# Two-layer conditioned transformer in float32: layer 1's modulation moved into the set-up, layer 0's feed-forward weights converted behind tile 0's attention, two PSUM banks for the last tile's chunks

## What is computed

```python
def layer0(x, cond):                       # modulated block with gates
    y = layernorm(x) * (1 + cond @ g1_w + g1_b) + (cond @ b1_w + b1_b)
    x = x + attention(y) * tanh(cond @ a1_w + a1_b) * 0.1
    z = layernorm(x) * (1 + cond @ g2_w + g2_b) + (cond @ b2_w + b2_b)
    return x + (gelu(z @ fc1_w + fc1_b) @ fc2_w + fc2_b) * tanh(cond @ a2_w + a2_b) * 0.1

def layer1(x, cond, mask):                 # shift, scale = split(cond @ ada_w + ada_b)
    h = layernorm(x) * (1 + scale1) + shift1
    q, k = rotary(h @ wq + bq), rotary(h @ wk + bk)
    x = x + masked_attention(q, k, h @ wv + bv) @ wo + bo
    h = layernorm(x) * (1 + scale2) + shift2
    return x + gelu(h @ ff_w1 + ff_b1) @ ff_w2 + ff_b2
```

## Time and profile before

| | |
|---|---|
| median of 3 runs | 2088.32 us (2086.74 to 2089.87) |
| the profiled execution | 2085.85 us, span 2084.0 us |
| mean granted TensorE clock | 0.971 of full |
| busy share of the span | PE 89%, PEld 80%, ACT 63%, DVE 60%, POOL 41% |

### The profile page before, as it was taken

One profiled execution on the slowest core, in us unless ns is written; L12 is line 12 of the kernel. 1 busy time (PEld: TensorE's weight loads), 2 busy tenths in 40 slices (PEclk: granted clock), 3 DMA queues, 4 the chain that ended last, 5 costly groups with the idle time before them and its releaser, 6 DMA issues.

```text
span 2084.0 us, 41504 instructions
## 1 busy us (share of the span) xinstructions
PE 1845.1 (89%) x12623; PEld 1664.0 (80%) x12623; DVE 1240.7 (60%) x2973; ACT 1319.0 (63%) x2315; POOL 849.9 (41%) x1036
## 2 busy tenths in 40 slices
PE   4789999999999999997877898888988889888897
PEld 4678888888888888886876888878888788887786
DVE  5566666666666666666653656546655466554651
ACT  3457667776667767775655566666666656656563
POOL 1214333333333333334444445554445544455433
PEclk8899999999999999999998999999999999999999
DMA  6454443333444444343431323223333233332220
GB/s 166 96 128 115 119 121 94 98 98 103 111 117 112 113 121 114 90 103 97 134 92 46 95 83 96 76 75 96 84 92 84 67 96 86 91 86 66 87 62 31
DMA packets 324131, 199.83 MB, mean 96 GB/s; under 512 B 158946, under 2 KB 312548, under 8 KB 324068
## 3 DMA queue, kind: packets, MB, share of 16 engines
q1 hardware_dynamic: 324068, 199.06, 35.7%
HBM read 80.98 MB, written 17.33 MB: 47 GB/s over the span
## 4 chain that ended last, share of the span: by engine, by line
PE 45%; issue 22%; ACT 8%; POOL 6%; DVE 6%; SPq 6%; DMA 5%; POOLq 1%; ACTq 0%; DVEq 0%
PE D L885 10%; PE C L885 9%; PE A L885 7%; PE B L1035 6%; PE B L885 6%; PE B L1021 3%; DMA x_res<-in_x 3%; ACT x_in L682 2%; POOL h_lo L550 2%; SPq L321 2%; ACT hact L739 2%; DMA rotation<-rotation 2%; ACT v_blocks L734 1%; SPq L418 1%; POOL rotation L590 1%
## 5 line engine op out<-in xcount | busy, mean ns | idle before, releaser
L550 POOL TENSOR_TENSOR h_lo<-hact,h_hi 128x512 fp32r<-128x512 f32 x256 | 330.6, 1291 | 341.1 <-ACT h_hi L744 332.6
L885 PE MATMUL D<-wgt_hi,h_hi 128*128 128x256 f32 x1024 | 305.4, 298 | 29.3 <-POOL h_lo L550 22.9
L885 PE MATMUL C<-z_hi,wgt_hi 128*128 128x512 f32 x512 | 218.6, 427 | 106.8 <-ACT hact L739 104.8
L885 PE MATMUL D<-wgt_hi,h_lo 128*128 128x256 f32 x1024 | 291.7, 285 | 0.0
L885 PE MATMUL D<-wgt_lo,h_hi 128*128 128x256 f32 x1024 | 291.2, 284 | 0.0
L885 PE MATMUL A<-k_pad,q_pad 128*128 128x256 f32 x1536 | 259.8, 296 | 12.3 <-DVE exps L1340 5.5
L1035 PEld LDWEIGHTS B<-v_blocks,probs_turned 128*128 128x128 f32 x2048 | 262.2, 201 | 7.1 <-ACT probs_turned L753 2.5
L1035 PE MATMUL B<-v_blocks,probs_turned 128*128 128x68 f32 x2048 | 266.5, 280 | 0.0
L739 ACT ACTIVATE hact<-C,b_col 128x512 f32<-128x512 f32 x256 | 176.4, 689 | 113.7 <-PE C L885 111.3
L1334 DVE TENSOR_REDUCE mx<-A 128x8 f32<-128x512 f32 x256 | 174.3, 681 | 115.7 <-PE A L1007 61.2
L885 PEld LDWEIGHTS D<-wgt_hi,h_hi 128*128 128x128 f32 x1024 | 198.9, 194 | 42.2 <-POOL h_lo L550 20.1
(11 more groups left out here) (138 smaller groups left out, 4258.0 us busy)
## 6 DMA issues: line engine op xcount, KB each, us to landing
k_pad<-k_flat SPq DMA_DIRECT2D x512, 64.0 KB, 2.0
q_pad<-q_flat SPq DMA_DIRECT2D x256, 128.0 KB, 2.3
gates<-gates SPq DMA_DIRECT2D x64, 256.0 KB, 4.3
x_bias<-x_bias SPq DMA_DIRECT2D x32, 512.0 KB, 3.5
rotation<-rotation SPq DMA_DIRECT2D x128, 128.0 KB, 2.1
x_in<-in_x SPq DMA_DIRECT2D x16, 512.0 KB, 3.9
gates<-gated_bias SPq DMA_DIRECT2D x32, 256.0 KB, 4.9
x_res<-in_x SPq DMA_DIRECT2D x16, 512.0 KB, 4.5
```

The lines of the kernel that those rows point to most:

```text
L550: pool.tensor_tensor(hb[1][:, m % 2, :], hact[:, m % 2, :], hb[0][:, m % 2, :].bitcast(F32), ALU.subtract).then_inc(h_lo, 1)
L885: ins = nc.tensor.matmul(dst, l, r, start=first_start and n == 0, stop=last_stop and n == len(todo) - 1, **kw)
```

## The change

Four edits are made together.

1. Layer 1's modulation. SP loads the two `ada` matrices and their eight columns in `begin` (into the last third of `rotation` and into `zn`, free until then), and PE and DVE compute layer 1's scales and shifts in `second`. `third` loses them on SP, PE and DVE.
2. Layer 0's feed-forward weights. SP issues their two loads (1 MB each) in `second` and no longer in `begin`. ACT and DVE convert them in `third`, after step 0, and no longer in `second`. PE waits for them ahead of the first `hidden` and `back` of tile 0 in step 1.
3. Set-up order. ACT converts the weights of queries, keys and values ahead of its wait for the modulation, the projection's right behind; DVE likewise in `begin`; ACT's tanh of the gates stands ahead of tile 1's normalisation; POOL clears `q_pad` in DVE's place.
4. The last tile. Its odd chunks go to bank A[0], and `last_chunks` writes `hidden(m)` ahead of `back(m-1)`; `hidden(m)` waits for the gelu of chunk m-2.

```diff
@@ build
-        ada_raw = [rot[:, n * TE:(n + 1) * TE].rearrange("p (k n) -> p k n", k=KC) for n in range(2)]
+        ada_raw = [buf.rearrange("p (k n) -> p k n", k=KC) for buf in (rot[:, 2 * TE:3 * TE], zn_buf[:, :])]
+        def hidden_bank(tile, m):
+            return A[0] if known(tile) and tile == 2 * NT - 1 and m % 2 else C
@@ SP begin
-                ld(w_in[2], w_raw[1].rearrange("p (k n) -> p k n", k=KC), rows(w[0]["fc1_w"]))
-                ld(w_in[3], w_raw[2].rearrange("p (k n) -> p k n", k=MC), rows(w[0]["fc2_w"]))
                 ld(mask_in, mask_u8[:, :], t["mask_BxS_bf1"])
+                for n in range(2):
+                    ld(mods_in[2], ada_raw[n], rows(w[1][f"ada{n + 1}_w"]))
+                    columns(mods_in[2], 1, n, [w[1][f"ada{n + 1}_b"][D:2 * D], w[1][f"ada{n + 1}_b"][0:D]])
@@ SP second
                 ld(rows_out, mask_rows, mask_add)
+                ld(w_in[2], w_raw[1].rearrange("p (k n) -> p k n", k=KC), rows(w[0]["fc1_w"]))
+                ld(w_in[3], w_raw[2].rearrange("p (k n) -> p k n", k=MC), rows(w[0]["fc2_w"]))
                 sp.wait_ge(rows_out, 80)
@@ SP third
-                sp.wait_ge(w_lo[2], 1)
-                for n in range(2):
-                    ld(mods_in[2], ada_raw[n], rows(w[1][f"ada{n + 1}_w"]))
-                    columns(mods_in[2], 1, n, ...)
                 qk_columns(1, [w[1]["bq"], w[1]["bk"]])
@@ ACT
             def begin():
                 first_norm(0)
+                high_weights(0, 0)
                 act.wait_ge(mod_done, 8)
                 first_columns(0, 0)
-                high_weights(0, 0)
+                high_weights(1, 0)
                 act.wait_ge(bias_in[0], NBIAS[0])
             def second():
-                high_weights(1, 0)
                 act.wait_ge(pe_gates, 1)
                 nc.scalar.activation(hact[:, 1, :], C[:, :], ACT.Tanh).then_inc(gates_tanh, 1)
+                first_norm(1)
+                first_columns(1, 0)
+                act.wait_ge(mod_done, 16)
+
+            def third():
                 high_weights(2, 0)
                 high_weights(3, 0)
-                act.wait_ge(mod_done, 16)
-
-            def third():
                 act.wait_ge(mod_done, 32)
                 act.wait_ge(bias_in[1], NBIAS[1])
@@ PE
             def second():
                 modulations(Dk[1], mod_raw[2], mod_raw[3])
+                pe.wait_ge(mods_in[2], 16 * 10)
+                pe.wait_ge(mod_done, 8)
+                modulations(Dk[0], ada_raw[0][:, :, D:2 * D], ada_raw[0][:, :, 0:D])
                 ...
+                pe.wait_ge(mod_done, 16)
+                modulations(Dk[1], ada_raw[1][:, :, D:2 * D], ada_raw[1][:, :, 0:D])
             def third():
-                ...
-                pe.wait_ge(w_lo[2], 1)
-                pe.wait_ge(w_lo[3], 1)
             def hidden(tile, m):
+                if known(tile) and tile == 2 * NT - 1:
+                    pe.wait_ge(gelu, upto(tile, MC, max(m - 1, 0)))
+                    pe.wait_ge(s_sub, upto(tile, 2 * G, 2 * G))
+                else:
+                    await_(pe, gelu, upto(tile, MC, m))
+            def last_chunks(tile):
+                hidden(tile, 0)
+                hidden(tile, 1)
+                for m in range(2, MC):
+                    back(tile, m - 2)
+                    hidden(tile, m)
@@ DVE
                 modulations(0, 0)
                 low_weights(0, 0)
+                low_weights(1, 0)
             def second():
-                low_weights(1, 0)
                 ...
-                low_weights(2, 0)
-                low_weights(3, 0)
+                dve.wait_ge(mods_in[2], 16 * 10)
+                for n in range(2):
+                    dve.wait_ge(pe_mods, 3 + n)
+                    modulations(1, n)
                 dve.wait_ge(rows_out, 80)
+
+            def third():
+                low_weights(2, 0)
+                low_weights(3, 0)
                 dve.wait_ge(bias_in[1], NBIAS[1])
```

More of the change, by code:

```diff
@@ L512, in begin @@
                 first_rstd(0)
-                for buf in kpad:
+                for buf in kpad + qpad:
                     pool.memset(buf[...].bitcast(F32), 0.0).then_inc(pad_zero, 1)
@@ L738, in hidden @@
                 await_(act, h_lo, upto(tile, MC, m - 1))
-                nc.scalar.activation(hact[:, m % 2, :], C[:, :], ACT.Gelu, bias=b1_col[:, layer, m:m + 1]).then_inc(gelu, 1)
+                nc.scalar.activation(hact[:, m % 2, :], hidden_bank(tile, m)[:, :], ACT.Gelu, bias=b1_col[:, layer, m:m + 1]).then_inc(gelu, 1)
             def hidden_high(tile, m):
@@ L867, in step @@
                     values(u + 1, 1)
-                if n is not None:
+                if n is not None and not (known(u) and u == -1):
                     first_norm(u + 2)
@@ L929, in third @@
             def third():
-                pe.wait_ge(mods_in[2], 16 * 10)
-                pe.wait_ge(mod_done, 16)
-                for n in range(2):
-                    modulations(Dk[n], ada_raw[n][:, :, D:2 * D], ada_raw[n][:, :, 0:D])
                 pe.wait_ge(mod_done, 32)
                 pe.wait_ge(gates_tanh, 1)
-                pe.wait_ge(w_lo[2], 1)
-                pe.wait_ge(w_lo[3], 1)
             def first_turn(tile, pair, attn):
@@ L1058, in hidden @@
                 if m == 0:
-                    if known(tile) and tile == NT:
-                        pe.wait_ge(w_lo[2], 2)
+                    if known(tile) and tile % NT == 0:
+                        pe.wait_ge(w_lo[2], tile // NT + 1)
                     pe.wait_ge(z_hi, upto(tile, 2, 2))
                     pe.wait_ge(z_lo, upto(tile, 2, 2))
-                await_(pe, gelu, upto(tile, MC, m))
-                product(C[:, :], [(w(W_FF1, FF, k, m * P, P), [zb[q][:, k, :] for q in range(2)]) for k in range(KC)])\
+                if known(tile) and tile == 2 * NT - 1:
[3 more added lines that the diff above has]
+                    await_(pe, gelu, upto(tile, MC, m))
+                product(hidden_bank(tile, m)[:, :], [(w(W_FF1, FF, k, m * P, P), [zb[q][:, k, :] for q in range(2)]) for k in range(KC)])\
                     .then_inc(pe_f1, 1)
@@ L1068, in back @@
                 if m == 0:
-                    if known(tile) and tile == NT:
-                        pe.wait_ge(w_lo[3], 2)
+                    if known(tile) and tile % NT == 0:
+                        pe.wait_ge(w_lo[3], tile // NT + 1)
                     await_(pe, f2_read, upto(tile, 2, 0))
@@ L1098, in step @@
                     back(u - 2, MC - 1)
+                if known(u) and u == 2 * NT:
+                    last_chunks(u - 1)
+                    return
                 if b is not None:
@@ L1216, in begin @@
                 nc.vector.memset(ones[:, :], 1.0).then_inc(consts_ready, 1)
-                for buf in qpad:
-                    nc.vector.memset(buf[...].bitcast(F32), 0.0).then_inc(pad_zero, 1)
                 dve.wait_ge(pe_mods, 1)
```

8 lines of the change are left out of this document (1 added, 7 removed).

## The result

The changed kernel takes **2106.47 us** (median of 6 runs, 2102.4 to 2112.51), the kernel before 2089.1 beside it (6 runs, 2086.74 to 2092.99). The ratio is 1.0084, 95% interval 1.0066 to 1.0102: slower by 17.4 us. The forecast was 2101.0, range 2096 to 2107.

What follows compares the result with a forecast made beforehand. PE, busy 89%, was taken to bound the loop steps, and SP's serial issue the start of step 1. Terms 17.5 - 3.3 + 1.0 - 2.5 = +12.7 gave 2098.6, plus 2.5 for the median: 2101.0 us, range 2096 to 2107.

Steps and rivals of the forecast that it cites:

- forecast's own case: Whole kernel: the four parts as summed, +9 to +17 us, 2097 to 2105; chance 0.80.
- part 1: Step 0 to step 1: SP waits on `w_lo[3]`, delaying keys, queries and biases; restart from 114.2 to 131.7, +17.5 us.
- part 3: Tile 0's attention: the moved 2 MB of weights delay transfers behind them, idle rings taking most; +1.0 us.
- the slow issue: SP's bias issues: one took 1.59 us where neighbours take 0.64; expected gone without the `ada` transfers, 0.95 us off.
- rival B: SP at `w_lo[3]`: not held, so the missing issues count; restart at 107.9, -11.1 us, 2077.2; chance 0.04.
- Part 2: Set-up: earlier casts and tanh, conversions gone, layer 1's modulation added; tile 0's first maximum at 47.1, -3.3 us.
- rival A: Tile 0's attention: all 6 us of the moved 2 MB stall group 2's queries; +15.4 us, 2103.7; chance 0.11.
- Part 4: Last tile: two banks and the new order shorten first `hidden` to last `back` from 28.0 to 25.4; -2.5 us.
- C: Passage to step 1: issues overlap or the step catches up, about no change; +4 us, 2092; chance 0.05.

Runs made afterwards that it cites:

- e1: The changed kernel with SP's first `x_bias` loads and their wait on `w_lo[3]` moved from step 0 to behind the biases; 2088.21 us, ratio to before 0.9996.
- r1: The changed kernel unaltered, run again for a second profile; 2107.61 us, ratio to before 1.0084.
- e2: The changed kernel with layer 0's two feed-forward loads issued in `begin` again, conversions and wait staying moved; 2103.44 us, ratio to before 1.0072.
- e3: The changed kernel with `q_pad` cleared by DVE again and not by POOL; 2107.09 us, ratio to before 1.0081.
- e8: e1 with layer 1's first weights (queries, keys, values, projection) issued in SP's step 0 behind `x_in`; 2079.99 us, ratio to before 0.9950.
- e6: e1 with `q_pad` cleared by DVE, and the feed-forward loads and 22 biases issued in SP's step 0 behind `x_in`; 2079.15 us, ratio to before 0.9947.
- e9: e6 with layer 1's first weights also issued in SP's step 0, as in e8; 2076.9 us, ratio to before 0.9929.
- e10: e9 with the wait on `w_lo[3]` and its two `x_bias` loads moved behind group 2's queries in step 1; 2070.1 us, ratio to before 0.9906.
- e4: The kernel before with only the last tile's edit (two banks and the new order); 2086.32 us, ratio to before 0.9990.
- e7: e1 and e2 together: SP not held by `w_lo[3]`, feed-forward loads issued in `begin` again; 2083.14 us, ratio to before 0.9966.
- e11: e10 with 64 unread PE products ahead of tile 1's first scores; 2081.22 us, ratio to before 0.9957.
- e12: e10 with 36 unread PE products behind tile 1's first scores; 2069.83 us, ratio to before 0.9909.

## Why the prediction was right, and where it was off

The direction and the main mechanism were right, the range held narrowly: the median came 5.5 us above the predicted time, inside the range by 0.5, and above the forecast's own case (2097 to 2105, chance 0.80). Two terms were too small, the chain in part 1 and the +1.0 of part 3. The range holds their sum only by the width taken in for other cases; that it does so by 0.5 us is luck.

- *Part 1, SP held by `w_lo[3]`: shown.* The profile has SP's idle stretch, the order of the issues and the releaser as forecast, and e1, which takes away only the hold, takes away the loss. Its 18.3 us next to the forecast's 17.5 are no confirmation of the size, though: 17.5 is net of the `ada` issues and the slow issue. By the prediction's own numbers the hold alone moves the restart from 107.9 to 131.7, 23.8 us; measured are 24.4 (r1) and 27.5. A kernel without the hold was priced at 2077.2 (rival B), and e1 takes 2088.21: its restart came at 110.66 and not near 107.9, 4.0 us were lost in step 1, and 4.7 in the stretch where layer 1 begins (below). The term that was too small is the chain from the release to the restart: forecast 26.1, measured 28.0 (110.19 to 138.20) and 28.4 in r1. I had taken 0.95 off for the slow bias issue; it came back (1.45 where its neighbours take 0.59), `rtab` took 3.9 us to land and not 3.3, and from the release to the first bias it was 9.9 and not 9.4.
- *Part 2, the set-up: right in size, wrong in what carries it.* First maximum at 47.38 and 45.94 (forecast 47.1). I put the gain to the conversions taken off DVE. e2 has them off too and still starts at 50.29: with the `ada` loads in the set-up, the gain needs the 2 MB out of their way. The claim that clearing `q_pad` on POOL does no harm was not safe, since DVE stands while POOL clears (last section), though e3 shows nothing in the median.
- *Part 3, the transfers: the step that failed, though the forecast as a whole held.* "I take +1.0" was to cover it; measured from the first maximum to the end of step 0 it is 56.4 - 48.7 = 7.7 us in the first profile, 54.2 - 48.7 = 5.5 in r1 (45.94 to 100.16). The other executions with the loads there agree: 5.6 in e1 and e8, 6.9 in e3. Only 5.36 and 3.21 of it are PE's wait for the queries, and in e1 1.87. PE's granted clock is 0.55 from 60 to 65 us in the first profile and 1.00 there before, but from 50 to 55 it is the other way round (1.00 and 0.50), so how the rest divides between late landings and the clock is not shown. That the loads cause it is: in e6, e9 and e10, which have them behind `x_in`, the same stretch takes 48.6, 48.7 and 48.4. So parts 2 and 3 together left step 0 ending 1.0 (r1) to 4.6 us later and not 2.3 sooner. My reasoning was that the idle rings from 42 to 48 us would take most of the 2 MB. They did take it, at up to 437 GB/s, but gates, keys and `x_res` queued up behind, and the stretch that follows ran at some 200 GB/s with the rings busy in every slice. This is rival A, which I gave 0.11; even it had the stall at 3.3 + 0.4 = 3.7 us where 5.5 to 7.7 came.
- By the Trainium skill, "DMA: Bandwidth & Descriptors", section "Queues, rings and completion order", each DMA engine takes its descriptors in ring order. The profile agrees: the 2 MB, issued at 42.74 and 43.21, have landed at 48.6 and 52.3, and the first gates, issued at 43.83, at 53.1. The same sentence of the page adds that a later transfer may still finish its write before an earlier one, so the prediction's "nothing issued after these 2 MB could land before them" goes beyond it; here the strict reading was the better guide than the mean load of the rings.
- *Part 4, the tail: right.* 25.18 us against the forecast 25.4, and e4 alone gives 2.4 us against 2.5.
- *The sum.* With r1: step 0's end +1.0, the restart at 135.01 - 114.22 = +20.8, tile 3's `x_in` +21.6, the first `hidden` of the last tile at 2072.60, +23.0; -2.8 in the tail: 20.2, as the spans differ. Before's profiled execution was 3.3 us under its median of 2089.1, which leaves 16.9 of the measured 17.4.
- *Rivals B and C*: SP's idle stretch refutes B. C is refuted by the median, and nothing of the delay is won back in the loops, whose steps stay at 58.1 us.

What is left open: single executions of one program differ by up to 10.7 us (e7). The profiles differ by up to 6.4 us between 946 and 1230 us, where layer 1's first weights are converted and the granted clock of single steps varies (0.89 in e8's first such step to 0.95 before). The same step, as a window of before and then of e1:

```profile
946.00:1018.00 72.00, 58.19 (x396) 52.46 (x396) 43.96 (x103) 42.17 (x74) 31.78 (x38) 0.95 0.33 91
```

```profile
946.40:1021.75 75.35, 62.00 (x396) 55.76 (x396) 43.98 (x103) 41.98 (x74) 31.69 (x38) 0.91 0.32 88
```

The work is the same 396 matmuls and the step is 3.3 us longer at the lower clock. What decides it I did not test. Against before this stretch cost +3.5 in the first profile of the change, +1.5 in r1, +4.7 in e1, +4.0 in e7, +5.5 in e8, +1.3 to +1.7 in e2, e3, e6 and e9, +3.2 in e11, +0.1 in e10, +0.2 in e4 and -1.0 in e12. The first profile and r1 are one program and differ by 2.0, so part of it follows the execution; whether part follows the edits is not shown, with one profile of each kernel.

## What to carry to other kernels

A wait in the program of an in-order engine holds everything written behind it, so when a producer is moved later, look up every wait on its semaphore and move each down to just ahead of its real consumer: here one such wait cost 18 us, and with it moved and the loads issued in SP's idle time the kernel became 1% faster than the one before. A prefetch is free only where nothing urgent is issued behind it before it has drained: the moved 2 MB and the 1 MB of layer 1 each delayed the next group's queries, and neither stopped PE behind `x_in`. It costs twice, the load of the rings and the issuing engine's own time; for the 1 MB the second was the larger (2.7 us against 1.7). The mean load of the rings does not show this; the time from issue to landing of the small transfers behind does.

## What the hardware showed that I had not expected

- While POOL clears buffers, a DVE instruction that reads and writes SBUF (`TENSOR_SCALAR`, 128x128) stands. DVE and then POOL in the first profile of the change:

```profile
12.99 3.81 DVE L1223 TENSOR_SCALAR mod<-mod,ln_col 128x128 f32<-128x128 f32 x1
17.15 0.28 DVE L1223 TENSOR_SCALAR mod<-mod,ln_col 128x128 f32<-128x128 f32 x1
...
13.01 1.86 POOL L517 MEMSET q_pad<- 128x1024 f32 x2
14.80 1.92 POOL L518 MEMSET v_blocks<- 128x2176 f32 x1
```

The instruction of 0.28 us takes 3.81 and ends at 16.80, 0.08 after the memset of `v_blocks`. In e3 the same one takes 2.27 and ends at 15.07, again 0.08 behind that memset; in r1 the two take 0.68 and 0.55, and the second ends at 14.62, 0.09 behind `q_pad`'s. The kernel before has it too, with `q_pad` on DVE: 1.73 us, ending 0.08 behind its memset of `v_blocks`. The same operation with its input in PSUM, at 12.08, takes 0.35 while `k_pad` is cleared, and the `TENSOR_TENSOR` conversions behind it run at full speed while `v_blocks` is cleared in r1. The Trainium skill, "SBUF — State Buffer", section "Who interferes with whom", has this as an exclusive lock on ports that POOL shares with DVE's two-port modes, which `tensor_scalar` can enter, and the trace agrees. At the first use of `mod_tile` the two profiles of the change are 2.57 us apart (19.89 and 17.32), at tile 0's first maximum 1.44 (47.38 and 45.94), so the stall is enough to explain that difference.

- PE's granted clock after a gap: with 8.88 us idle ahead of it, groups of six took 1.62 us each; with the gap filled, 0.95. It cost 1.7 us of a step here.
